# Two moves in an early-fusion transformer kernel: which tile of the elastic feed-forward's norm is taken first, and in which token group the last feed-forward turns its last tiles

## What is computed

```python
h = _L0_tok_ref(x, ...)                      # patches -> 64 tokens of 192
h = jnp.concatenate([h, txt], axis=1)
h = h + _L0_attn_ref(_layernorm(h), ...)     # one head, grouped weights
h = h + _L0_ffn_ref(_layernorm(h), ...)      # 12 heads, then the elastic feed-forward
h = h + _L1_attn_ref(_layernorm(h), ...)     # 4 experts x 12 heads, window of 64, gated
h = h + _L1_ffn_ref(_layernorm(h), ...)      # the last feed-forward
```

```python
# elastic: samples 0-7 at full width, samples 8-15 a weighted sum over widths 192, 96 and 64
h = jax.nn.gelu(xp * cmask @ w1 + b1)        # 192 -> 768
return (h @ w2 + b2) * cmask                 # 768 -> 192
# last
h = jax.nn.gelu(x @ in_weight.T + in_bias)   # 192 -> 768
out = h @ out_weight                         # 768 -> 192
```

## Times and profile before

| | us |
|---|---|
| median of three runs | 1114.33 |
| the three runs | 1117.25, 1114.33, 1114.12 |
| profiled execution | 1112.48 |
| its span in the profile | 1110.8 |
| mean granted clock of TensorE, share of full speed | 0.993 |
| TensorE busy | 1069.5 (96% of the span) |
| ScalarE busy | 763.2 (69%) |
| VectorE busy | 722.5 (65%) |
| GpSimd busy | 570.6 (51%) |

### The profile page before, as it was taken

One profiled execution on the slowest core, in us unless ns is written; L12 is line 12 of the kernel. 1 busy time (PEld: TensorE's weight loads), 2 busy tenths in 40 slices (PEclk: granted clock), 3 DMA queues, 4 the chain that ended last, 5 costly groups with the idle time before them and its releaser, 6 DMA issues.

```text
span 1110.8 us, 34055 instructions
## 1 busy us (share of the span) xinstructions
PE 1069.5 (96%) x13103; PEld 868.9 (78%) x13103; DVE 722.5 (65%) x2256; ACT 763.2 (69%) x3370; POOL 570.6 (51%) x859
## 2 busy tenths in 40 slices
PE   6999998999999999999999999999999999999998
PEld 4788886777777465358888888888888888888577
DVE  8666566666766214367887878888888878877201
ACT  2356556777787435548988889888888888887231
POOL 2156666454455676436655465565465565465200
PEclk9999998999999999999999999999999999999999
DMA  8100603000000000010000000000000000000000
GB/s 273 29 5 2 135 3 79 1 2 1 2 1 1 1 1 1 1 51 2 3 3 3 2 3 3 3 3 3 3 2 3 3 3 2 3 3 3 11 22 32
DMA packets 35056, 19.66 MB, mean 18 GB/s; under 512 B 24656, under 2 KB 32336, under 8 KB 34896
## 3 DMA queue, kind: packets, MB, share of 16 engines
q1 hardware_dynamic: 34752, 17.00, 5.8%
q10 hardware_dynamic: 144, 0.49, 0.1%
HBM read 14.93 MB, written 1.77 MB: 15 GB/s over the span
## 4 chain that ended last, share of the span: by engine, by line
PE 88%; DVE 6%; ACT 3%; POOL 1%; issue 1%; DVEq 0%; POOLq 0%
PE banks L1750 8%; PE banks L1821 8%; PE banks L1758 6%; PE banks L1837 5%; PE banks L1532 5%; PE banks L1809 4%; PE banks L1856 4%; PE banks L2202 3%; PE banks L1814 3%; PE banks L2156 3%; PE banks L505 2%; PE banks L1258 2%; PE banks L1279 2%; PE banks L1861 2%; PE banks L1797 2%; PE banks L1844 2%
## 5 line engine op out<-in xcount | busy, mean ns | idle before, releaser
L2123 POOL TENSOR_TENSOR e_W<-e_W,e_RS 128x384 f32<-128x384 f32 x256 | 205.2, 827 | 233.0 <-DVE e_RS L1997 230.8
L1947 ACT ACTIVATE e_W<-banks,e_MX 128x128 f32<-128x128 f32 x768 | 270.1, 371 | 18.1 <-DVE e_MX L1983 18.1
L1947 ACT ACTIVATION_READ_ACCUMULATOR e_W<-banks,e_MX 128x1 f32 x768 | 161.2, 210 | 0.0
L1750 PE MATMUL banks<-XT,e_wqk 64*128 64x141 f32 x744 | 119.2, 295 | 0.0
L1750 PEld LDWEIGHTS banks<-XT,e_wqk 64*128 64x128 f32 x744 | 96.3, 188 | 18.1 <-issue 16.6
L1758 PE MATMUL banks<-e_wv,XT 128*128 128x192 f32 (+3 forms) x512 | 109.9, 344 | 0.6 <-DVE e_PT L2001 0.6
L1821 PE MATMUL banks<-ident,e_W 128*128 128x128 f32 x768 | 106.1, 274 | 1.1 <-POOL e_W L2123 0.8
L1506 POOL TENSOR_TENSOR f_W<-f_W,e_RS 128x423 f32<-128x423 f32 x64 | 56.3, 892 | 90.0 <-DVE e_RST L1485 79.7
L1941 ACT COPY e_PT<-banks 128x512 f32<-128x512 f32 x128 | 68.9, 588 | 40.6 <-PE banks L1821 40.3
L1983 DVE TENSOR_REDUCE e_MX<-banks 128x3 f32<-128x384 f32 x128 | 65.4, 552 | 41.4 <-PE banks L1809 41.4
L1821 PEld LDWEIGHTS banks<-ident,e_W 128*128 128x128 f32 x768 | 87.5, 143 | 2.3 <-DVE e_V L2010 1.0
(11 more groups left out here) (328 smaller groups left out, 2724.2 us busy)
## 6 DMA issues: line engine op xcount, KB each, us to landing
xp<-in_patches_dram SPq DMA_DIRECT2D x4, 768.0 KB, 9.2
H<-in_h_dram SPq DMA_DIRECT2D x1, 1728.0 KB, 13.2
out_dram<-H SPq DMA_DIRECT2D x6, 288.0 KB, 2.3
m_hid<-in_e_gu_dram SPq DMA_DIRECT2D x1, 1536.0 KB, 9.2
m_hid<-in_e_o_dram SPq DMA_DIRECT2D x4, 192.0 KB, 6.9
e_wqk<-in_e_qk_dram SPq DMA_DIRECT2D x8, 96.0 KB, 2.5
e_wqk<-in_e_qk_dram SPq DMA_DIRECT2D x24, 32.0 KB, 2.3
tokw<-in_tok_w_dram SPq DMA_DIRECT2D x1, 576.0 KB, 5.2
```

What stands on the lines that cost most here:

```text
L1750: return nc.tensor.matmul(bank[6][:, m * SEQ:(m + 1) * SEQ], ew[n % EXPERTS][0][0:rows_c, c, m * P:(m + 1) * P], XT[0:rows_c, c, tokens(n) ...
L1947: ex = nc.scalar.activation(W[n % 2][:, t, :], bank[i][:, x * P:(x + 1) * P], ACT.Exp, bias=MX[:, t:t + 1], accum_out=SM[n % 2][:, t:t + 1])
L2123: nc.gpsimd.tensor_tensor(x, x, RS[n % 2][:, 3 * i:3 * i + 3].unsqueeze(2).broadcast_to([P, 3, P]), ALU.mult).then_inc(s_nm, 1)
```

## The change

Three moves, and no instruction added or taken away.

1. In the elastic feed-forward ScalarE copies tile 17 (alone in bank 7) first, then 15 and 16. `wide_down` uses the banks the other way round, 7 for even tiles and 6 for odd ones; its first product waits for one copy only (`IN_F + 1` is 16, with the 15 earlier ones counted), its second for all three. VectorE's additions read the swapped banks.
2. In the last feed-forward `back_rest` moves from behind up(0) into up(1), between first and second halves.
3. There `forward_rest` moves from up(2) into up(3), with its wait raised from three to six finished tiles. ScalarE's copies move from behind group 1's gelus to behind group 2's, and the wait for them from the first two down products of group 1 to those of group 2.

```diff
@@ wide_down
                             if t >= 2:
                                 pe.wait_ge(s_mfn, t - 1)
                             else:
-                                pe.wait_ge(s_nev, T3 + TILES)
+                                pe.wait_ge(s_nev, T3 + (IN_F + 1 if t == 0 else TILES))
                             for m in range(HM):
-                                mm = nc.tensor.matmul(bank[6 + t % 2][:, 0:C], m_hid[g % 2][:, m, j * P:(j + 1) * P],
+                                mm = nc.tensor.matmul(bank[7 - t % 2][:, 0:C], m_hid[g % 2][:, m, j * P:(j + 1) * P],
@@ elastic, ScalarE
-                            for k, i in enumerate(range(IN_F, TILES)):
-                                evacuate_third(act, REST3_AT[k], i, TILES - 1)
+                            for k in (2, 0, 1):
+                                evacuate_third(act, REST3_AT[k], IN_F + k, TILES - 1)
@@ finish_wide, VectorE
-                            nc.vector.tensor_tensor(H[:, t, :], bank[6 + t % 2][:, 0:C], H[:, t, :], ALU.add
+                            nc.vector.tensor_tensor(H[:, t, :], bank[7 - t % 2][:, 0:C], H[:, t, :], ALU.add
@@ last feed-forward, up
                             up_part(g, m, 0, 0, P, True, False)
-                        if g == 2:
+                        if g == 1:
+                            back_rest()
+                        if g == 3:
                             forward_rest()
                         for m in range(HM):
                             up_part(g, m, 1, m % 2 * C1, C1, False, True).then_inc(s_up, 1)
-                        if g == 0:
-                            back_rest()
@@ forward_rest
-                        pe.wait_ge(s_fn, 3)
+                        pe.wait_ge(s_fn, 6)
@@ down
-                            if g == 1 and j < 2:
+                            if g == 2 and j < 2:
                                 pe.wait_ge(s_nev, T5 + TILES)
@@ last feed-forward, ScalarE
-                        if g == 1:
+                        if g == 2:
                             act.wait_ge(s_nft, T5 + TILES)
```

## The result

| | before | changed |
|---|---|---|
| median, us | 1114.55 (4 executions, 1114.12 to 1117.25) | 1102.34 (4 executions, 1101.19 to 1106.28) |
| profiled execution, us | 1112.48 | 1101.19 |
| its span, us | 1110.8 | 1099.5 |
| mean granted clock of TensorE | 0.993 | 0.999 |

The ratio is 0.9892 with a 95% interval of 0.9862 to 0.9922. The direction was right and the size wrong. At the places where the edits act the forecast was nearly exact; what it missed lies in the stretches of lower clock and in its starting point.

A forecast was written before the change was run, and what follows sets the result against it. TensorE, 88% of the chain that ended last, was taken as the bound, so only its idle or slow stretches could win. 4.44 + 0 + 1.88 = 6.32 us off the 1114.33 us median gave 1108.0 us, range 1105.6 to 1110.6.

The forecast's parts named there:

- Part 1: Last feed-forward: back transposes inside group 1's up products win 4.44 us (2.50 idle, 0.51 transposes, 1.43 clock).
- the 1.5 us of slack: Last feed-forward: GpSimd's gated product is ready 1.5 us before TensorE reaches the moved transposes.
- Part 2: Last feed-forward: turning the norm's last three tiles one group later wins 0; bounds 0.16 us less, 0.2 us more.
- Part 3: Elastic feed-forward: copying bank 7's tile first starts the first down product 1.89 us earlier; 1.88 us won.
- rival C: First expert unit: the shift moves the spell at 497; 1106.7 us if it goes (0.08), 1109.3 if another comes (0.02).
- The anchor: Whole kernel: the sum is subtracted from 1114.33 us, the median of the runs shown, giving 1108.0.
- 1.1 us for the spread of a median: Whole kernel: allowance below 1106.7 us that sets the range's lower end at 1105.6 us.
- A: Last feed-forward: slow spell comes anyway or was absent from timed executions; only 4.8 us won, 1109.6; chance 0.06.
- B: Elastic stage: its 1.88 us are given back before the experts; 4.4 us won, 1109.9; chance 0.06.
- E: Expert stage: another rhythm makes the kernel slower, by over 0.3% from 0.16 us a unit on; chance 0.03.

The follow-up runs named there:

- only_last: The kernel before with only the last feed-forward's two moves, the elastic edit left out: 1105.23 us (ratio 0.9944), in a repeat 1106.11 us (0.9955).
- only_back: The kernel before with only the back transposes moved into group 1's up products, forward transposes left in group 2's: 1106.62 us in its one execution.
- gap_filled: The kernel before with nine throwaway identity products in the last stage's 2.50 us gap on TensorE: 1108.37 us (ratio 0.9976).

## Why the prediction was wrong

The forecast missed by 5.7 us. Two steps failed: the time from which the sum was taken (3.4 us), and the price of the elastic gap, in which the sum put the clock at nothing (1.3 to 1.7 us in most executions). By its own steps:

- **Part 1, the backward turn: right.** 4.44 us forecast, 4.40 measured; up to down is 12.92 to 12.94 us in every trace with the move. The four transposes, the 1.5 us of slack ahead of them and the full clock came as written. Filling the gap showed the clock's share: 1.5 to 1.6 us, for 1.43 in the up products and 0.51 in the transposes; the idle and the rest are 2.9. The total was better than its split.
- **Part 2, the forward turn: right.** 0, and the stall of 0.16 us moved with it.
- **Part 3, the elastic edit: right at its place, wrong in what it costs elsewhere.** 1.90 us for 1.88. The failed step is the sentence "This gap costs its length and nothing beyond". It was read from the earlier trace rows of one trace; the sum held no clock for it. All seven traces with this idle have a spell behind it, right there (93.96 us to the masks in place of 92.3: 1.7 us) or in the first expert unit (9.6 us in place of 8.35: 1.3 us), and the ten without it have none at either place. The term is 1.90 + 1.3 to 1.7, near 3.3 us, where a spell falls; of the 26 executions of only_last, only_back and gap_filled, which all keep this idle, 5 had a clock of 1.000 and so paid 1.90 alone. The earlier trace rows showed the spell, and the forecast made of it rival C, with 0.08 for winning it. That half of C came in every trace of the kernels with the elastic edit, so 0.08 was far too low. Whether its cause is the shift, as C has it, or the idle, is open; the spell right at the gap is the idle's.
- **The anchor.** The sum was taken from the 1114.33 us of three executions. Over all 104 executions of before that the comparisons made, the median is 1110.93 and the mean 1111.40 (1107.36 to 1117.27). So 3.4 of the 5.7 us by which the forecast missed are the starting point's, the larger of the two failed steps. The profile told of it: its mean clock of 0.993 is at the low side of what the kernel shows (mean 0.995), and the spell at 183, 3.2 us long in cost, was not looked for, because the clock was read only around the touched stretches. "1.1 us for the spread of a median" was far too little for a median of three.
- **The rivals.** A (no spell at the last gap) did not come in any trace, but in the four executions of the elastic edit alone at 1103.90 to 1104.20 us; its 1.55 us stands beside the sum's 1.43 without a working. B did not come: the expert stage begins 2 us earlier. From the second unit's transposes to those of the 62nd, sixty units on, are 499.10 us, as before (499.08); so no E.

Where the spell falls, the parts make 1.9 + 1.3 to 1.7 + 4.4 = 7.6 to 8.0 us. The means of all executions differ by 8.06 (1111.40 and, over 19 of the changed kernel, 1103.34), the medians by 9.06 (1110.93 and 1101.87). The means agree, as far as 19 executions tell that scatter by 2.8 us. The same by the clock: a straight line through the times against the clock puts before at 1106.0 and the changed kernel at 1100.5 at full clock, 5.4 apart (the idle and what hangs on it are 1.9 + 2.9 = 4.8), and the mean clock rises from 0.9949 to 0.9976, which at 1.03 us for 0.001 is another 2.8. The single kernels fit less well: the last stage's edits alone win 5.8 us in the mean (1105.62, 15 executions) for 4.4 at their place, and the elastic edit alone 1.8 (1109.58, 24 executions), for 1.9 + 1.3 to 1.7 less the 1.4 to 1.6 of the longer spell. The 1.4 us too much in the first are open; executions without a trace may have longer spells at the last gap than the traces show.

Why the first four executions of before all took over 1114 us, where of the other 100 only 18 do, is not settled: chance or that chip. A spell ahead of unchanged code, as at 38 and at 183 us, comes in 4 of 17 traces. Here the Trainium skill (TensorE: Matmul & The Clock Gate, Part 1, What's actually happening) agrees: it says that the gate's watch isn't tied to the kernel's start and that the same kernel shows a different number of slow matmuls from run to run. It adds that the penalty of the ramp to full speed is under one per cent of a typical kernel and not to be fitted to a count. The size agrees, but not its harmlessness: the 10 us between the fastest and the slowest execution are 0.9% of the time, and more than the change brings.

## What to carry to other kernels

Price an idle stretch of TensorE of two microseconds as its length and a likely spell of lower clock behind it, even where the one trace at hand shows none, and say how likely. Look at the small gaps of later stages too: whether a spell falls there can change with the edit. Before a forecast takes a median of a few executions as its base, read the mean granted clock, list every stretch below full clock in the whole span, and ask what the kernel would take without those that hang on nothing. When an edit's ratio comes out as "no change", compare distances between the same instructions in both traces: within a stage and between traces without a spell there they were good to 0.05 us, over the 378 us from the start to 0.2, where medians of a dozen executions moved by 1. When an experiment is to tell two causes of a spell apart, first make sure from the clock records that the traces compared stand alike.

## What the runs showed of the hardware

- A gap of 2.50 us on TensorE, in a stream otherwise full, had a spell at half clock behind it in 4 of 4 traces, one of 1.89 us right behind it in 2 of 7. Filling 2.27 us of the first with products of the identity kept the clock at 1.00, and so did 2.05 us of them in the second. Neither gap has a spell in every execution: by their mean clock 4 of 24 went without at the first, 5 of 26 at the second and behind it.
- Spells came in lengths near 3.4, 6.8 and 10.2 us. 3.4 us cost 1.3 to 1.7 us, 6.8 us cost 3.2.
- Two gaps of 0.93 and 0.79 us, 95 us behind the elastic gap, had a spell in five of the seven traces with the elastic gap idle, and in none of the eight without that idle in which they are unfilled. Whether the earlier idle or the place of the small gaps decides is not explained by any run here.
- A spell can begin with no idle ahead (at 38 us, twice).
- The clock's first rise came at 14.9 to 17.5 us in twelve traces and at 21.1 to 21.4 us in five, which cost those 1.4 us: a transpose of 128 columns took 421 ns ahead of it and 273 ns behind.
- Four transposes between matmuls cost no clock (1.00 from 1020 to 1034 us).
